# A two-layer block on one core: the shared expert's products as plain float32, its output copied by ScalarE, the routed rows sent eight in a row

## The reference

```python
# layer 0: x is (2, 512, 256); 16 heads of 16
xn = _layernorm(x)
s = _L0_attn_ref(xn, Wq, Wk, Wv, Wo, o_norm_w)   # rotary q and k, 4 key blocks of 32 chosen per query,
                                                  # softmax, rms norm of every head, output projection
g = _silu(_L0_ffn_ref(xn, gate_w, w_gate, w_up, w_down, sw_gate, sw_up, sw_down))
x = x + s * g

# inside _L0_ffn_ref: 8 experts of 176 hidden units, 2 for each token, and one shared expert of 352
scores = softmax(x @ gate_w); topk_w, topk_idx = top_k(scores, 2)
routed = sum over the chosen experts of topk_w * (silu(x @ w_gate[e]) * (x @ w_up[e])) @ w_down[e]
shared = silu(x @ sw_gate) * (x @ sw_up) @ sw_down
out = routed + shared

# layer 1: a gated linear recurrence (width 320) for s, a selected low-rank edit for g
```

## Time and profile before

| | |
|---|---|
| median of 3 runs | 406.1 us (405.85 to 408.53) |
| the profiled execution, its own time | 409.56 us |
| its span, first to last instruction | 407.7 us |
| granted clock of TensorE, mean | 0.908 of full speed |
| busy: PE, DVE, ACT, POOL | 77%, 68%, 40%, 30% |
| layer 1 begins at | 303 us |

### The profile page before, as it was taken

One profiled execution on the slowest core, in us unless ns is written; L12 is line 12 of the kernel. 1 busy time (PEld: TensorE's weight loads), 2 busy tenths in 40 slices (PEclk: granted clock), 3 DMA queues, 4 the chain that ended last, 5 costly groups with the idle time before them and its releaser, 6 DMA issues. The chain is left out here.

```text
span 407.7 us, 5771 instructions
## 1 busy us (share of the span) xinstructions
PE 313.8 (77%) x1762; PEld 203.5 (50%) x1762; DVE 279.1 (68%) x865; ACT 164.7 (40%) x332; POOL 122.7 (30%) x105
## 2 busy tenths in 40 slices
PE   0699638567578799899899999994625998995981
PEld 0487527455344455555555555542614784444741
DVE  3857799986489778777234444447839969378694
ACT  1413611451012223232665656562303676938510
POOL 2555545577002111111113434445145000000123
PEclk9999897988588899999999999999685898998898
DMA  8992377456998374755443424015017000000011
GB/s 276 307 287 62 103 166 213 128 149 229 247 183 175 105 178 115 207 161 149 111 143 93 127 77 118 0 29 181 0 33 240 0 2 0 0 0 2 0 51 51
DMA packets 52545, 47.88 MB, mean 117 GB/s; under 512 B 5282, under 2 KB 50204, under 8 KB 52509
## 3 DMA queue, kind: packets, MB, share of 16 engines
q1 hardware_dynamic: 50211, 42.12, 38.7%
q0 software_dynamic: 1872, 4.22, 3.0%
q10 hardware_dynamic: 432, 1.18, 1.0%
HBM read 35.44 MB, written 15.87 MB: 126 GB/s over the span
## 5 line engine op out<-in xcount | busy, mean ns | idle before, releaser
L501 POOL DMA_INDIRECT yt_dram<-ysb,x x23 | 23.0, 1001 | 117.5 <-ACT ysb L617 78.9
L673 ACT ACTIVATE PT<-bank 128x512 f32<-128x512 f32 (+1 forms) x88 | 44.9, 559 | 21.5 <-PE bank L1177 20.8
L889 DVE TENSOR_REDUCE mx<-bank 128x1 f32<-128x384 f32 (+3 forms) x88 | 52.2, 636 | 1.5 <-PE bank L1159 0.8
L1158 PE MATMUL bank<-KS,QS 112*128 112x128 bf16 (+3 forms) x128 | 34.9, 319 | 12.3 <-DVE mx L889 10.7
L1788 PE MATMUL lbank<-u,w_ai 128*128 128x512 f32 x72 | 33.0, 619 | 1.9 <-issue 1.9
L1176 PE MATMUL bank<-QS,KS 115*128 115x512 bf16 (+3 forms) x128 | 31.0, 302 | 2.7 <-ACT PT L673 1.1
L1491 POOL TENSOR_TENSOR left<-xn,x 128x256 f32<-128x256 f32 x8 | 6.9, 897 | 85.9 <-DVE xn L1718 85.9
L1032 DVE SCALAR_TENSOR_TENSOR s<-th,bank 128x176 f32<-128x176 f32 x23 | 7.7, 336 | 33.7 <-ACT th L705 33.6
L507 POOL TENSOR_TENSOR small<-small,mhalf 128x16 f32<-128x16 f32 x8 | 24.4, 3046 | 17.3 <-DVE small L935 17.3
L1158 PEld LDWEIGHTS bank<-KS,QS 112*128 112x128 bf16 x128 | 12.7, 100 | 31.0 <-DVE mx L889 26.5
L1159 PE MATMUL bank<-tri,ident_b 128*128 128x128 bf16 x128 | 25.6, 227 | 0.0
(11 more groups left out here) (280 smaller groups left out, 807.8 us busy)
## 6 DMA issues: line engine op xcount, KB each, us to landing
wr<-w_dram SPq DMA_DIRECT2D x12, 352.0 KB
wt<-w_dram SPq DMA_DIRECT2D x11, 352.0 KB
QS<-parts_dram SPq DMA_DIRECT2D x12, 256.0 KB
KS<-parts_dram SPq DMA_DIRECT2D x12, 256.0 KB, 5.2
xs_dram<-x SPq DMA_DIRECT2D x1, 2967.0 KB, 15.4
x<-xs_dram SPq DMA_DIRECT2D x23, 129.0 KB, 2.8
w_dram<-in_w_chunks_dram SPq DMA_DIRECT2D x11, 256.0 KB, 4.8
wr<-in_w_chunks_dram SPq DMA_DIRECT2D x12, 176.0 KB
```

The source lines that it names most:

```text
L501: pool.indirect_dma_start(yt_dram, bass.IndirectOffsetOnAxis(ap=xg[:, n % XBUF, D:D + 1].bitcast(I32), axis=0), ysb[:, n % 2, :], None, bo ...
L673: act.activation(PT[:, k % 8, 0:n], bank[k % 2][:, 0:n], ACT.Exp, scale=float(DH) ** -0.5).then_inc(P_ready, 1)
L889: dve.tensor_reduce(mx[:, b * TB + i, heads[0]:heads[-1] + 1], bank[k % 2][:, 0:len(heads) * n].rearrange("p (h n) -> p h n", n=n), AX.X, ...
L1158: pe.matmul(out, QS[0:R_MAX, b, h, i * P:(i + 1) * P], KS[0:R_MAX, b, h, 0:n], start=True, stop=False)
```

## The change

Six things are done.

1. The weights of the shared expert are no longer split: ACT's queue loads all three chunks at the start into `ws` (float32), and the casts and subtractions that made `wh` and `wl` are gone.
2. An unsplit copy of the transposed input, `xT`, is made by ACT in four copies from banks 0 to 3, each after DVE's `xl` of that bank. It lies in a part of `KS` that is stacked with k of sequence 1 later, so SP's stacking waits for the last `up_product`.
3. `gate_product`, `up_product` and `down` are one float32 matmul where there were three of float32r; `gb` has two buffers and isn't split (`gh`, `gl` are gone).
4. `take_y` moves from DVE to ACT.
5. POOL sends the eight tiles of a choice in a row, ahead of its slots in step 1 and step 3, instead of four after its slots in each of steps 1 to 4. `second_choice` moves to the end of DVE's step 2.
6. The routed tiles 0 and 1 can load their weights into `wr` without a wait, since no chunk has been there.

```diff
@@ sizes and buffers
-CHUNK_LOADS = [2, 1, 0, 0]
+SEND_STEP = [1, 3]
-        wh = early.sb("wh", [P, SCH, 3, 256], F32R)
-        wl = early.sb("wl", [P, SCH, 3, 256], F32R)
+        ws = early.sb("ws", [P, SCH, 3, 2 * P])
+        xT = KS[:, 1, 6:14, :].bitcast(F32).rearrange("p (k h) t -> p k (h t)", k=KD)
@@ SP
                 first = sp.value_load(expert[0:1, n:n + 1], min_val=0, max_val=(E - 1) * EH)
-                if n < 2:
-                    sp.wait_ge(wh_ready, SCH - n)
-                    sp.wait_ge(wl_ready, SCH - n)
-                else:
+                if n >= 2:
                     sp.wait_ge(down_done, SHARED + max(n - WBUF + 1, 0))
...
                     sp.wait_ge(parts_out[n % 4], 48 * (b + 1))
+                    if which and b:
+                        sp.wait_ge(U_ready, SHARED)
@@ POOL
-            split_chunk(0)
...
             for s in range(SHARED):
-                if s + 1 < SCH:
-                    split_chunk(s + 1)
-                for q in step_slots(s)[0:2]:
+                for k in range(EK):
+                    if s == SEND_STEP[k]:
+                        pool.wait_ge(pad_in, 16)
+                        pool.wait_ge(routed, LABELLED[k])
+                        for t in range(T):
+                            send_rows(k, t)
+                for q in step_slots(s):
                     slot(q)
-                pool.wait_ge(gh_ready, s + 1)
-                if s >= 2:
-                    pool.wait_ge(down_done, s - 1)
-                pool.tensor_tensor(gl[:, s % 2, :], gb[:, :], gh[:, s % 2, :].bitcast(F32),
-                                   ALU.subtract).then_inc(gl_ready, 1)
-                for q in step_slots(s)[2:]:
-                    slot(q)
-                if 1 <= s <= 4:
-                    k = (s - 1) // 2
-                    if s == 1:
-                        pool.wait_ge(pad_in, 16)
-                    pool.wait_ge(routed, LABELLED[k])
-                    for t in range((s - 1) % 2 * TB, (s - 1) % 2 * TB + TB):
-                        send_rows(k, t)
@@ ACT
-            load_chunk(0)
-            load_chunk(1)
+            for c in range(SCH):
+                act.dma_start(ws[:, c, :, :], a["w_chunks"][ECH + c]).then_inc(ws_in, 16)
...
+            for n in range(2 * B):
+                b, c = n // 2, n % 2
+                act.wait_ge(xl_ready, n + 1)
+                act.copy(xT[:, c, b * S:(b + 1) * S], bank[n][:, :]).then_inc(xT_copied, 1)
...
-                act.wait_ge(g_ready, s + 1)
-                if s >= 2:
-                    act.wait_ge(down_done, s - 1)
-                act.copy(gh[:, s % 2, :], gb[:, :]).then_inc(gh_ready, 1)
-                for q in qs[2:]:
+                for q in qs[1:]:
                     slot(q)
+                if s == SCH:
+                    take_y(0)
...
+                if i == 0:
+                    take_y(1)
@@ DVE
-                if s == SCH:
-                    second_choice()
                 for q in qs[1:]:
                     slot(q)
                 if s == 0:
                     expert_places()
-                if s == SCH:
-                    take_y(0)
+                if s == SEND_STEP[1] - 1:
+                    second_choice()
@@ PE
                 for k in range(KD):
-                    ins = split_matmul(pe, bank[3][:, :], wh[:, w, k, 0:P], wl[:, w, k, 0:P],
-                                       xh[:, k, part], xl[:, k, part], k == 0, k == KD - 1)
+                    ins = pe.matmul(bank[3][:, :], ws[:, c, k, 0:P], xT[:, k, part], start=(k == 0), stop=(k == KD - 1))
...
-                    ins = split_matmul(pe, bank[6 + k][:, o * D:(o + 1) * D],
-                                       gh[:, s % 2, tokens(2 * k + o)], gl[:, s % 2, tokens(2 * k + o)],
-                                       wh[:, c, 2, :], wl[:, c, 2, :], c == 0 and o == 0, c == SCH - 1, skip=True)
+                    ins = pe.matmul(bank[6 + k][:, o * D:(o + 1) * D], gb[:, s % 2, tokens(2 * k + o)], ws[:, c, 2, :],
+                                    start=(c == 0 and o == 0), stop=(c == SCH - 1), skip_group_check=True)
```

100 lines of the change are left out of this document (35 added, 65 removed).

## The result

| | before | after |
|---|---|---|
| median, 18 runs each on one chip | 406.12 us | 404.65 us |
| the profiled execution, its own time | 409.56 us | 407.62 us |
| its span | 407.7 us | 405.8 us |
| busy: PE, DVE, ACT, POOL | 77%, 68%, 40%, 30% | 78%, 67%, 40%, 27% |
| layer 1 begins at | 303.4 us | 300.6 us |

Ratios compare only the fast runs of each kernel, those within 1.5% of its fastest, which sets aside seven of the eleventh kernel's twelve runs and few of any other, and the profiled execution of the change is one of its slower ones, so that its trace is read for places and not for its total.

What follows compares the result with a forecast made beforehand. DVE was taken to set the pace in the shared expert's steps, then PE to wait for the gathered rows. Transposes −1.6, float32 +0.2 and `take_y` −1.2 made −2.6 us, thus 403.5 us against the median 406.1; range 400.0 to 408.0.

Steps and rivals of the forecast that it cites:

- The opening, +1.1 us: At the start, loading the third weight chunk delays `wp` and the projection by 1.1 us, bounds 0 and +1.3.
- Float32 on PE: Shared expert: one float32 matmul for three float32r adds 5.6 us of PE work, nearly all under DVE's; +0.8 us on the path.
- DVE's gain, 4.3 us: Without POOL's subtractions, DVE ends step 2 4.3 us earlier than 78.93 us, bounds 2.5 and 5.
- The new wait, 9 us: DVE stands 9 us before `R1` of part 6, as L of part 4 follows the second eight sends on POOL.
- The rows: SP's read of gathered rows goes out at 98.6 us with the opening, instead of 103.17, and lands at 104.7.
- The transposes, −1.6 us: PE begins the transposes of gathered rows at 107.7 us instead of 109.27; its 4.25 us wait for rows is gone.
- `take_y`, −1.2 us: Step 6: the second copy on ACT leaves the path between `select` and DVE's maxima, −1.2 us, bounds −1.3 and 0.
- After step 6, +0.2 us: Float32 in step 6 and after costs 0.2 us, in part.
- The gain did not come through: Rival: the gain comes through, with DVE saving 5 us in steps 0 to 2 and a free opening; −5.2 us, 400.9 us; chance 0.2.
- The slower case: Rival: the port gives DVE only 1 us, the second row of sends starts 3.3 us later; 408.0 us; chance 0.15.
- No copy was held by the sends: Rival: sends hold DVE's cast, `bias` conversions and label copies, DVE loses 1.4 us; 404.9 us; chance 0.06.
- The clock rival: PE stands from about 82 to 90 us, then works at 1.2 GHz until after step 5; +1.5 us, 405.0; chance 0.12.

Runs made afterwards that it cites:

- eleventh kernel: The kernel with sends four and four, rows' read and weights of tiles 2 and 3 moved up, third chunk late, given sends eight in a row again: 0.9886.
- best kernel: The changed kernel with sends four and four, rows' read ahead of stacking q, weights of tiles 2 and 3 ahead of k, third chunk later: 396.44 us, 0.9765.
- doubled products: The changed kernel with every gate and up product of the shared expert computed twice: 407.16 us, 1.0002.
- The first: The changed kernel with the second row of sends one step later, in step 4 instead of 3: 404.64 us, 0.9921.
- fourth kernel: The changed kernel with sends four and four in steps 1 to 4 again and `second_choice` back in step 3: 402.22 us, 0.9849.
- seventh kernel: The kernel before with part 5 of the change alone, eight sends in a row in steps 1 and 3: 415.22 us, 1.0189.
- second experiment: The changed kernel with both copies of `y` (`take_y`) back on DVE at their old places: 408.07 us, 0.9978.
- twelfth kernel: The kernel before with only SP's queue reordered: rows' reads ahead of stacking q's second half, weights of tiles 2 and 3 ahead of k: 404.54 us, 0.9911.

## Why the prediction was right, step by step

What the parts are worth can be read from six kernels, by the ratio to before and by the start of layer 1:

| | copies of `y` on DVE | copies of `y` on ACT |
|---|---|---|
| float32, sends four and four | 0.9858, 296.9 us | 0.9849, 298.0 us |
| float32, sends in a row | 0.9978, 303.4 us | 0.9942, 300.6 us (the change) |
| split operands, sends in a row | 1.0189, 309.9 us | not run |
| split operands, sends four and four (before) | 1, 303.4 us | not run |

So the float32 form (with its operands' loads and `xT`) is worth 1.4%, and the row of sends takes 0.9 to 1.2% back with it. ACT's copies give 2.8 us at layer 1 when DVE is late (the 0.4% of the ratios lie within their intervals) and nothing that shows when it is not. The forecast had a small net from large terms of both signs, and these are they.

That the ratios and the places don't agree everywhere has a reason that the prediction left out. It took layer 1, whose code is the same in all, as adding nothing either way. In the profiled executions layer 1 takes 100.4 to 105.2 us, with the same instructions and a different granted clock (length, busy PE, PEld, DVE, ACT, POOL, clock, DMA share, GB/s; before and the best kernel):

```profile
303.36:407.70 104.34, 80.65 (x270) 50.67 (x270) 79.47 (x168) 53.52 (x89) 12.74 (x13) 0.86 0.11 37
```
```profile
293.45:393.80 100.35, 77.09 (x270) 49.35 (x270) 76.38 (x168) 53.41 (x89) 12.96 (x13) 0.91 0.12 39
```

That is more than the whole gain of the change. It doesn't go with the edits in an order that I can name (105.2 us with the change, 101.4 with `y` on DVE), and what sets it is open. So small differences of ratios say less about layer 0 than the start of layer 1 does.

- **The opening, +1.1 us: right.** 0.9 to 1.0 in the trace. The cause is shown: ACT's cast of `wp` begins at 11.62 to 11.84 us in the seven kernels that load three chunks at the start, and at 10.71 to 11.02 in the other seven. (By its own numbers the lower rate is 0.33 MB/us and not 0.31, which makes the upper bound 1.2.)
- **Float32 on PE: right in kind.** 1.88 us with its tail for four records of a product, as worked out (1.72 and a tail). That it is covered is what the doubled products show: of 20.6 us more, at most 2.5 reached the end. I had put 0.8 of 5.6 on the path; the same share, 0.12, would give 0.7, an estimate, since the doubled kernel leaves `down` as it was and works at a higher clock.
- **DVE's gain, 4.3 us: mis-sized.** 78.93 − 74.54 is 4.4 us, and with the later opening 5.4. The scan, the 184 elements and the cast gave 1.6, 0.9 and 0.96, as forecast. `R1` of part 2 gave 1.2 (start and length) instead of 0.9. The term that I left out is `R1` of part 3, which had taken 1.58 us in the kernel before and takes 0.69: there L of part 2 had begun 0.18 us ahead of it, at 51.28, and here L of part 2 begins 0.13 us behind it, at 51.34, so DVE goes first. A small shift of the order was worth 0.9 us, as much as a subtraction removed. That the port and nothing else gave these microseconds is argued from the lengths; no run takes only POOL's subtractions away.
- **The new wait, 9 us: right.** 9.93. Eight sends took 10.16 us from the first's begin to the last's end; DVE went on at 87.15, against 86.4 to 87.5 plus the opening. The last `kmb` ended at 92.1, with the opening 0.2 us over the 90.9 + 1.0. Errors cancelled here: step 2 ended 1.1 us sooner than forecast, but the first send began 0.84 us after `second_choice` where 0.15 had been put, and eight sends took 10.16 us where the forecast had them end after 10.0 (its 10.2 and its 85.1 don't fit together). The first, fourth, seventh and eleventh kernels show the cause: the stand is 9.93 us wherever the row of eight stands ahead of L of part 4, and absent where it doesn't.
- **The rows: the time was right, the reason half so.** I had the read at 98.6; it was 99.19. I had it follow from L of part 5 by fixed distances. SP's queue was in fact late elsewhere: its `bias` columns took 6.3 us to come back (77.61 to 83.90; 2.2 us in the fourth kernel, 76.86 to 79.05), which pushed the weights and the parts behind it. Against that the parts landed in 3.0 us and not 4.7, and the stacking was issued in 3.9 and not 4.9, so the sum came out near. The delay is not the sends' as such: in the seventh kernel the same trip, from 84.46 to 86.74 in the midst of a row of eight, took 2.3 us, and in the first it took 4.7 us (76.14 to 80.85) with no send under way. In all kernels in which it was slow, SP had issued the stacking of k of sequence 0 until 1.4 to 2.6 us before it, here from 72.28 to 76.11, and the DMA engines were full (a share of 1.11 from 76 to 82 us); in the quick ones that stacking lay 5.8 us or more back. It stood so late because L of part 3 waits behind the first eight sends (68.19 us, where it was 56.28 before). I had given that stacking time until slot 20 and did not see what it would meet. This cause is argued from the order of the rows; no run moves the stacking alone. It cost nothing here, since PE came at 107.15 by DVE's chain.
- **The transposes, −1.6 us: right**, −2.1 in the trace (107.15 for 107.7); DVE's combination of step 5 came 2.7 us later than before (98.49 for 95.77), where 3.0 was forecast.
- **`take_y`, −1.2 us: the size was right, the place too narrow.** PE's wait fell by 1.5 us. But I had put the first copy "off the path" once ACT has it, and priced only the second. The second experiment gives 2.8 us for the two: the first would have cost 2.3 at `block_gates(1)`, as DVE's stand makes all that follows on it late. With ACT it was off the path only just: the `down` behind it began at 90.45 and took 1.84 us at the lower clock, until 92.29, and the last `kmb` was done at 92.09.
- **After step 6, +0.2 us: too small.** Behind the wait for the maxima PE was 3.4 us ahead of before (116.20 for 119.57), at layer 1 2.8. Some 0.6 us were lost in between; in which steps was not followed. A head start is not kept whole, though I had assumed that it is: the twelfth kernel has 6.0 us at the transposes and 3.5 at layer 1, the best 13.1 and 9.9.
- **The rivals.** The gain did not come through, for the reason given against it: L of part 4 behind the sends. The slower case needed a last `kmb` near 94; it ended at 92.1. No copy was held by the sends: the twelve conversions of `bias` took 0.23 us in the middle and 0.31 at most. The clock rival came true in part: the granted clock was 0.80 from 79 to 89 us and 0.55 from 89 to 96, after PE had stood for 8.31 us. From the start of `block_gates(1)` to that of the last gate product PE took 3.65 us (92.29 to 95.94), and 2.21 in the fourth kernel, where it did not stand: 1.4 us. The rest of step 5 then ran at the higher clock and gave 0.6 back.

What stays open: the seventh kernel lost 1.9% where the same row costs 0.9 to 1.2% with float32. By the start of layer 1 it costs 6.5 us in both forms as long as DVE copies `y` (303.4 to 309.9, and 296.9 to 303.4), and 2.6 with ACT's copies; so it need not be another cost, but with one trace of each this is not settled. And the best kernel's 0.9765 has the rows, the weights and the chunk together; the weights alone were not run.

## What to carry to other kernels

An engine that hands out transfers in a row holds all that stands behind it in its queue: before such a row is formed, look for who waits for the next item there (here L of part 4, then DVE, then PE), not at when the data it sends are wanted. The sends ended 7 us sooner than four and four (85.8 against 92.8) for nothing, since the reader was held by its own queue, and when it no longer was, by DVE's chain. When a wait on a transfer is removed and the time doesn't move, look in the same queue for what was pushed back: here the weights of tile 2, an 11.2 us wait; moved up with the rows (and with the chunk later), they gave the kernel its largest step. And when a change is worth less than the kernel varies in a part that it doesn't touch, compare the place where that part begins, beside the total.

## What the runs showed of the hardware

An indirect send of 128 rows holds GpSimd for 0.97 us, and the next begins 1.28 us after it. The first of a row of eight takes 1.16 to 1.22, and the second begins some 1.5 us after it. A row of eight took 10.1 to 10.2 us in every kernel that has one.

A small write to DRAM and its read on SP's queue took 2.2 to 2.3 us from issue to issue, also beside a row of such sends (the seventh kernel). It took 4.7 to 6.6 us where six stacking reads had been issued just ahead of it.

PE's granted clock rose with its load: from 60 to 69 us it was 0.94 with the change and 1.00 with the products doubled, and 20.6 us of added work cost at most 2.5. After PE had stood 8.31 us it was 0.55 from 89 to 96 us.

Layer 1, with the same 270 TensorE instructions in the trace, took 104.3 us at a mean granted clock of 0.86 in one profiled execution and 100.4 at 0.91 in another.
